# Adjacency cast to float16 by DRAM-to-DRAM DMA and turned by transposing DMAs, in a two-layer graph network on one core

## What is computed

```python
h = jnp.maximum(_layernorm(x, axis=-1), 0.0)
x = x + max_over_neighbours(h, adj)      # where(adj != 0, h, -inf), max over the 4096 nodes
h = jnp.maximum(_layernorm(x, axis=-1), 0.0)
g = h @ W                                # 4096 x 128 by 128 x 128
e = (g @ a1)[:, None] + (g @ a2)[None, :]
e = jnp.where(e > 0, e, 0.2 * e)
e = jnp.where(adj > 0, e, NEG)
x = x + elu(softmax(e, axis=1) @ g)
```

## Time and profile before

| | before |
|---|---|
| median of three timed runs | 742.38 us |
| the profiled execution's own time (its span, first to last instruction) | 753.0 us |
| TensorE busy | 681.6 us (91%) |
| VectorE busy | 693.7 us (92%) |
| ScalarE busy | 473.1 us (63%) |
| GpSimd busy | 281.8 us (37%) |
| DMA, mean over the span | 217 GB/s, 163.07 MB |
| HBM read, written | 117.51 MB, 44.56 MB |

### The profile page before, as it was taken

How to read it: one execution, slowest core, us unless ns; L and a number is a source line. 1 busy time by engine, 2 the same in 40 slices (tenths; PEclk the granted TensorE clock), 3 DMA queues, 4 the chain that set the end, 5 groups by cost and what they waited for, 6 DMA issues and landing times.

```text
span 753.0 us, 14749 instructions
## 1 busy us (share of the span) xinstructions
PE 681.6 (91%) x5560; PEld 490.6 (65%) x5560; DVE 693.7 (92%) x1023; ACT 473.1 (63%) x685; POOL 281.8 (37%) x259
## 2 busy tenths in 40 slices
PE   1788999999999999999999998699999999999994
PEld 1344655555555555555555554498998999999994
DVE  8999999999999999999999999988998999889893
ACT  3888999889898899998999897562433111001000
POOL 0612034434434535444444355441620294134040
PEclk9999999999999999999999999799999999999998
DMA  9999978997888888888888746342531544443400
GB/s 305 310 355 390 344 230 270 303 327 239 268 249 247 273 258 237 272 265 241 261 263 265 246 143 228 103 143 71 187 130 62 219 140 158 156 177 130 165 15 17
DMA packets 63000, 163.07 MB, mean 217 GB/s; under 512 B 6416, under 2 KB 11152, under 8 KB 58832
## 3 DMA queue, kind: packets, MB, share of 16 engines
q1 hardware_dynamic: 53776, 138.75, 54.2%
q0 software_dynamic: 9152, 23.34, 12.1%
HBM read 117.51 MB, written 44.56 MB: 215 GB/s over the span
## 4 chain that ended last, share of the span: by engine, by line
PE 53%; DVE 31%; issue 12%; ACT 2%; DMA 1%; DVEq 0%; another core or an unknown queue 0%; SPq 0%
PE pick_ps L714 23%; DVE acc L867 20%; PE pick_ps L613 17%; DVE rest L1054 5%; PE late_ps L627 4%; PE late_ps L585 4%; PE order_ps L594 2%; PE late_ps L693 1%; PE late_ps L623 1%; DMA best<-x 1%; DVE left L889 1%; ACT depth L403 1%; DVE found L915 1%; PE late_ps L714 1%; PE order_ps L680 1%
## 5 line engine op out<-in xcount | busy, mean ns | idle before, releaser
L867 DVE TENSOR_TENSOR acc<-pick_ps,acc 128x1024 f32<-128x1024 f32 x248 | 302.6, 1220 | 20.9 <-PE pick_ps L613 12.6
L363 POOL DMA_INDIRECT found<-subset_max,tops x192 | 204.4, 1065 | 271.8 <-DVE acc L867 187.5
L1054 DVE SCALAR_TENSOR_TENSOR rest<-depth,curves_sb,stage 128x512 f32<-128x512 f32 x256 | 199.5, 821 | 15.3 <-PE pick_ps L714 3.1
L714 PE MATMUL pick_ps<-keys,rest 128*128 128x129 f32 x1792 | 207.7, 276 | 3.3 <-DVE rest L1054 3.2
L714 PEld LDWEIGHTS pick_ps<-keys,rest 128*128 128x128 f32 x1792 | 204.6, 193 | 7.4 <-DVE rest L1054 5.8
L402 ACT ACTIVATE first<-order_ps 128x1024 f16<-128x1024 f32 x128 | 131.9, 1030 | 39.1 <-PE order_ps L594 33.0
L403 ACT ACTIVATE depth<-order_ps 128x1024 f16<-128x1024 f32 x128 | 131.5, 1027 | 0.0
L613 PE MATMUL pick_ps<-first,h_hi 128*128 128x512 f16 x256 | 97.3, 380 | 17.6 <-DVE acc L867 17.1
L613 PE MATMUL pick_ps<-second,h_hi 128*128 128x512 f16 x256 | 97.2, 380 | 15.2 <-DVE acc L867 14.7
L585 PEld LDWEIGHTS late_ps<-ident_h,stage 128*128 128x128 f16 x1024 | 68.4, 99 | 50.0 <-DMA stage<-adj 12.9
L613 PE MATMUL pick_ps<-first,h_lo 128*128 128x512 f16 x256 | 97.4, 380 | 0.0
(11 more groups left out here) (146 smaller groups left out, 599.9 us busy)
## 6 DMA issues: line engine op xcount, KB each, us to landing
stage<-adj SPq DMA_DIRECT2D x64, 1024.0 KB
edge_units<-edge_t SPq DMA_DIRECT2D x64, 512.0 KB
stage<-edge_units SPq DMA_DIRECT2D x32, 1024.0 KB, 4.8
subset_max<-keys POOLq DMA_DIRECT2D x13, 512.0 KB, 9.0
found<-subset_max,tops POOLq DMA_INDIRECT x192
best<-x SPq DMA_DIRECT2D x4, 512.0 KB, 5.9
subset_max<-x POOLq DMA_DIRECT2D x4, 512.0 KB, 6.6
out<-keys POOLq DMA_DIRECT2D x7, 256.0 KB, 2.8
```

Source lines behind the costliest of these rows:

```text
L363: nc.gpsimd.indirect_dma_start(found[:, n % NG, s, :], None, subset_max, bass.IndirectOffsetOnAxis(tops[:, n, s:s + 1], 0)).then_inc(gathe ...
L714: last = nc.tensor.matmul(out_ps(q, b), weight[:, n % WEIGHTS, b * P:(b + 1) * P], wh[:, c, :], start=c == 0 and starts(q, b), stop=c == C ...
L867: V.tensor_tensor(acc[:, q % 2, :], pick_ps[k][:, :], acc[:, q % 2, :], ALU.max).then_inc(raised, 1)
L1054: V.scalar_tensor_tensor(out=weight[:, n % WEIGHTS, :], in0=limit[:, q % 4, :], scalar=slope[:, c:c + 1], in1=units[:, m % EDGES, k * TI:( ...
```

## The change

The adjacency is no longer loaded as int32 and turned by TensorE. GpSimd issues DMAs that read 512 rows x 512 columns of the int32 adjacency from DRAM and write them as float16 to a new DRAM tensor `adj_h` (`cast_piece(q, i)`, eight pieces for each tile q of 512 targets). SyncE issues transposing DMAs that read 512 x 512 of `adj_h` and write it turned into one of eight slabs in SBUF (`turn(n)`, one for two steps). TensorE's `flip` and ScalarE's `edges` are gone, and so are the stores `keep`. For layer 1 SyncE turns 512 x 1024 of `adj_h` into each unit (`turn_unit(m)`) where it loaded a stored unit. The pieces of the first tile are issued at the start (two of them at once, six when x has landed), those of the second tile one behind each of the first eight table stores, those of the third tile one in each of the steps 11 to 18, and those of tile q + 3 two behind each group of fetches of tile q. VectorE's `rests` is gone as well: ScalarE's `later` now makes the rest mask of every step, and `digest` adds the word constant with its matmul in every group, not in every second one.

```diff
-        stage = sb("stage", [P, STAGES, ROWS, KCOLS], I32)
+        turned = sb("turned", [P, SLABS, KEEP * W], F16)      # SLABS = 8, KEEP = 2, KCOLS = 512
-        edge_t = sb("edge_t", [P, KEPT * KEEP, W], F16)
...
-        units = stage.rearrange("p s r k -> p s (r k)").bitcast(F16)
+        units = turned.rearrange("p (u t) k -> p u (t k)", t=SLABS // EDGES)
...
             def _(sp):
+                def turn(n):
+                    q, u = n // PER_TILE, n % PER_TILE
+                    sp.wait_ge(cast[q % 2][u * CASTS // PER_TILE], 16 * (q // 2 + 1))
+                    if n >= SLABS:
+                        sp.wait_ge(ordered, (n - SLABS + 1) * KEEP)
+                    sp.dma_start_transpose(turned[:, n % SLABS, :].rearrange("p (c t) -> p c t", t=TI),
+                                           adj_h[q * TI:(q + 1) * TI, u * KCOLS:(u + 1) * KCOLS]).then_inc(landed[n % SLABS], 16)
+
+                def turn_unit(m):
+                    q, u = LOADED[m] // UNITS, LOADED[m] % UNITS
+                    sp.dma_start_transpose(units[:, m % EDGES, :].rearrange("p (c t) -> p c t", t=TI),
+                                           adj_h[q * TI:(q + 1) * TI, u * UCOLS:(u + 1) * UCOLS]).then_inc(edge_in[m % EDGES], 16)
...
                 for n in range(LOADS):
-                    if n + STAGES < LOADS:
-                        sp.wait_ge(flipped, (n + 1) * KEEP)
-                        load(n + STAGES)
-                    keep(n)
+                    turn(n)
...
                 for m in range(EDGES, TILES * UNITS):
-                    at = LOADED[m]
                     sp.wait_ge(made, UNIT_END[m - EDGES] + 1)
-                    sp.dma_start(units[:, m % EDGES, :], edge_units[at * P:(at + 1) * P, :]).then_inc(edge_in[m % EDGES], 16)
+                    turn_unit(m)
...
             def _(pool):
+                def cast_piece(q, i):
+                    rows, cols = slice(q * TI, (q + 1) * TI), slice(i * N // CASTS, (i + 1) * N // CASTS)
+                    nc.gpsimd.dma_start(adj_h[rows, cols], adj[rows, cols]).then_inc(cast[q % 2][i], 16)
+
+                for i in range(EARLY):
+                    cast_piece(0, i)
+                for i in range(4):
+                    pool.wait_ge(x_in[i], 16)
+                for i in range(EARLY, CASTS):
+                    cast_piece(0, i)
                 pool.wait_ge(hs_ready, 4)
...
                     nc.gpsimd.dma_start(subset_rows(m), spare(i % 4)).then_inc(saved[i % 4], 16)
+                    if i < CASTS:
+                        cast_piece(1, i)
+                for i in range(CASTS):
+                    pool.wait_ge(raised, 2 * (len(CHAINS) + i))
+                    cast_piece(2, i)
                 pool.wait_ge(saved[3], 32)
...
+                    if n // ROWS + 3 < TILES:
+                        for i in range(CASTS // ROWS):
+                            cast_piece(n // ROWS + 3, n % ROWS * CASTS // ROWS + i)
...
             def _(act):
-                    if g + AHEAD - 1 < PAIRS:
-                        edges(g + AHEAD - 1)
                     if g % 2 == 0 and g >= 4:
                         key(g // 2 - 2)
                     if g + 3 < PAIRS:
                         select(g + 3)
-                    if g % 4 == 0:
-                        later(g + 2)
-                    elif g % 4 == 2:
+                    if g + 1 < PAIRS:
                         later(g + 1)
...
             def _(pe):
                     pick(g, 1)
-                    if g + AHEAD < PAIRS:
-                        flip(g + AHEAD)
                     if g >= 2:
                         digest(g // 2 - 1, g % 2)
...
             def _(dve):
                     take(g, 0)
-                    if g % 4 == 0:
-                        rests(g // 2)
-                    elif g % 2 and g + 1 < PAIRS:
+                    if g % 2 and g + 1 < PAIRS:
                         seconds(g // 2 + 1)
```

117 lines of the change are left out of this document (32 added, 85 removed).

## The result

| | before | after |
|---|---|---|
| median of four executions | 742.21 us | 787.67 us |
| fastest and slowest of them | 742.03, 742.62 us | 775.38, 804.13 us |
| ratio, with its 95% interval | | 1.051 [1.044, 1.058] |
| span of the profiled execution | 753.0 us, and 741.0 us in run b0 | 783.5 us |

The change makes the kernel 5% slower; 734 us was forecast. A ratio leaves out executions that are over 1.5% above the fastest of the same kernel, here two of the four after the change. I compare with that one from here on.

A forecast was written before the change was run, and what follows sets the result against it. VectorE was taken to bound layer 0 and TensorE layer 1. From the profiled 753.0 us, - 19.2 - 3 + 12 + 2 gave 744.8 us, times 0.986 the forecast 734 us; range 708 to 800 us, the forecast's own 712 to 740.

The forecast's parts named there:

- the start pays for the lead: Start of layer 0: VectorE's chains stall for table stores queued behind cast pieces and turns; 12 us added.
- The bytes up to table store 6: Start: 26.8 to 29.9 MB queued ahead of that store's landing, done at 78.5 to 87 us.
- the start eats all: Rival at the start: a stall of 20 to 38 us instead of 12, giving 742 to 760 us; chance 0.20.
- A slab at 2.4 us of DMA time: Turns in layer 0: each 512 KB slab costs 2.4 us of the DMA engines, half a unit load.
- The rival of slower turns: Both layers: turns slower than plain transfers, 4.8 us a slab and 9.6 us a unit, about 870 us; chance 0.16.
- Eight pieces ahead of the last two table stores at 0 us: Steps 11 to 18, GpSimd's queue: pieces ahead of these stores cost nothing; 9 us kept for the range.
- Masks 19.2 us, TensorE 3 us: Layer 0: 32 rest masks off VectorE at 0.60 us save 19.2 us; TensorE without transposes saves 3 us.
- The tile I forecast, 52 to 53.5 us: Middle of layer 0: a tile of 16 steps taking 52 to 53.5 us, named as a sign of being right.
- x later, 2 us: Start: two cast pieces share the DMA engines with x, delaying it 2 us, within 0 to 5 us.
- the 30 us that I had named as a sign of being wrong: Start of layer 0: a first maximum later than 30 us would show the prediction wrong.
- Layer 1, 0 us: Layer 1: a turned unit needed every 7.1 to 8.0 us is hidden at 4.8 us, costing 0 us.

The follow-up runs named there:

- b0: The kernel before the change, unedited, timed and profiled once more: 743.09 us, profiled span 741.0 us.
- e4: The changed kernel with each cast piece issued as two DMAs of 256 columns instead of one of 512: 789.65 us, ratio 1.060.
- e6: The changed kernel with layer 0's turns replaced by plain DMAs of the same bytes, edges not transposed there: 768.7 us, ratio 1.035.
- e10: The changed kernel with plain DMAs for layer 0's turns and the last two table stores ahead of the third tile's pieces: 752.46 us, ratio 1.013.
- e7: The changed kernel with half of the rest masks back on VectorE: 800.78 us, ratio 1.078.
- e1: The changed kernel with the third tile's cast pieces put behind tile 0's fetches and each later tile's one tile later: 774.3 us, ratio 1.032.
- e9: The changed kernel with the last two table stores issued ahead of the third tile's eight pieces: median 803.5 us, no usable ratio.
- e14: e12 with the second load of x moved to the end of layer 0: median 742.06 us of twelve, ratio 0.994.
- e15: e14 with one cast piece instead of two in four groups of fetches after step 30: 874.28 us, ratio 1.170.
- e12: First two tiles as before the change, their edges stored and loaded again; later tiles as in the changed kernel: 742.98 us, ratio 1.002.

## Why the prediction was wrong

The step that failed is the term "the start pays for the lead", 12 us. It put the whole stall at VectorE's chains behind the table stores, and it let the turned slabs come in time: TensorE's wait for them stood in the sum at nothing. The chains wait only 1.6 us. TensorE's rank waits 35.1 us for slabs, and ScalarE's first key 12.4 us for the last two table stores.

The bytes up to table store 6 were not the mistake. That store landed at 66.2 + 17.2 = 83.4 us, within the 78.5 to 87 us of the sum; its issue, and its time to landing:

```profile
66.17 0.54 POOL L338 DMA_DIRECT2D subset_max<-keys  x1 [4.10 <-DVE keys L811]
...
DMA to landing us min/median/max: 17.2/17.2/17.2
```

Nor were the engines much slower, if a piece is counted by what it reads, as in the prediction. From 60 to 100 us:

```profile
DMA packets 12336, 10.03 MB, mean 251 GB/s; under 512 B 7889, under 2 KB 11182, under 8 KB 12334
...
q1 hardware_dynamic: 7638, 1.92, 35.4%
```

The 3293 packets between 512 B and 2 KB are the pieces', 3.37 MB written. With as much again for the reads it is 13.4 MB in 40 us, 335 GB/s, against 343 in b0. What failed is who gets them: the turns got 1.92 MB, 3.7 slabs, one in 10.9 us, where two steps eat one in 6.5. For that share bytes were the wrong unit: a turn goes in packets of 252 bytes. Halving the casts' packets took the slabs' wait from 35.1 to 9.3 us (e4), and plain slabs took it away (e6). Plain slabs change the packets and the transposing at once; e4 changes packets alone, those of the casts. Where slabs come sooner the stall that I had described does appear: the chains wait 13.5 us in e4, 9.7 in e6 and 10.6 in e10, where I had 12. Why the turns were so slow from 119 to 133 us stays open.

The rival "the start eats all" had the place right, but for another reason, the written half of the casts. That 787.67 us lies in the wide range of 708 to 800 us is luck: the part of it above 760 us was drawn for casts and turns that cost time behind the start, where none was lost.

- *A slab at 2.4 us of DMA time* (half a unit load): right for layer 1, where 512 KB take 2.5 us. Beside casts, in the middle, 8.15 MB (15.5 slabs) took 60.9% of 100 us, 3.9 us each, and a turn landed in 12.4 us; plain ones took 25.0% for 16 slabs, 1.6 us. The rival of slower turns had such a price, 4.8 us, but for every slab and unit; in the middle and in layer 1 the turns are covered, and only the start, where nothing is in hand, pays.
- *Eight pieces ahead of the last two table stores at 0 us*, 9 us kept for the range: 12.4 us, in ScalarE's first key, and 21.5 us of TensorE's wait for that key in e6.
- *Masks 19.2 us, TensorE 3 us*: 1.6 us a tile against b0, which would be 13 us in eight tiles. The masks give all of it and TensorE nothing (e7). A mask is worth 0.4 us, not 0.60: the distance from its start to the next maximum is no price of taking it out. VectorE was already 97.5% busy before; the waits that I let the lighter TensorE buy were those of that one execution. The tile I forecast, 52 to 53.5 us, was right (52.04) by luck: I set out from 55.5 us, 1.85 too many, and took off too much.
- *x later, 2 us*: the first maximum comes at 31.45 us instead of 27.44 (b0), 4.0 us; within the bound of 5, and later than the 30 us that I had named as a sign of being wrong.
- *Layer 1, 0 us*: right. Turned units land in 6.0 us (median), and from the last fold to the end it takes 213.7 us (b0: 213.1):

```profile
L833 DVE TENSOR_TENSOR best<-acc x8: 681/683/684, 122.0 to 569.8; 128x512 f32<-128x512 f32 x8
```

In numbers against b0: 741.0 + 30.7 (first tile) + 21.1 (second) - 8.3 (five tiles of 1.66 us) - 1.0 (the rest) = 783.5 us.

The Trainium skill ("DMA: Bandwidth & Descriptors", Queues, rings and completion order) says that an engine goes round the queues that have work, one packet at a time; a packet there is a group of descriptors, and no run shows whether it is the packet that the trace counts. Had I weighed it, small packets beside large ones would have been a rival with a price of its own. Run e4 agrees with it. From 103 to 118 us, where almost only pieces and turns are in flight, the turns' 2304 packets go beside 2157 of the other queue, nearly one for one; from 70 to 100 us it is 6278 beside 3334, and from 119 to 133 us 2214 beside 143, which the rule doesn't explain.

The Trainium skill ("Advanced Engine Details and Errata", X-Bar Transpose (TRN2)) says that transposing DMAs are as fast as regular ones. Beside casts they are not: 12.4 us to land against 5.8 us for the same bytes (e10), and 2.4 times the engines' time. Alone a turn landed in 4.7 us (e1, 123 to 134 us); the quickest plain slab took 3.3 us (e6).

What stays open: why executions of the kernels that wait for turns differ so much (775 to 804 us after the change, 780 to 814 in e9), where those of e6 and e10 lie within 2 us; and whether e14's longer executions all lose in the third tile, since only one was profiled.

## What to carry to other kernels

A transfer that shares the DMA engines is costed by its packets as well as by its bytes, and beside the transfers that it will meet: count both, look at what each queue moves, not at the share alone, and see which side of a cast a profile counts. A stage in which nothing is in hand yet pays for each late transfer in full, so a change that is free in the steady state is judged by its first tiles; and where pieces are paced by the work itself, a lead that is taken away may not be won back (e15). Profile the kernel before twice if its span doesn't fit its times.

## What the runs showed of the hardware

The issue of a transposing DMA of 512 KB holds SyncE's queue for 5 to 18 us when the DMA engines are loaded (the stores and the load of x between the turns of e12 0.6 to 0.9 us), and for 1.9 to 2.5 us where nothing else is in flight (e1, 123 to 134 us). A plain slab's issue took 0.37 us in the median of e6, but 12.6 us once, right behind the second load of x; so a long issue is not a matter of transposing alone. Whatever stands behind a long issue on that queue, here a store or the next turn, is late as well. TensorE's granted clock fell to 0.72 to 0.79 in the stretches with long waits (e6: 0.72 from 100 to 140 us) and was 0.97 to 1.00 in the next stretch without them; what that added to the stalls was not measured apart.
